# Where the arithmetic of three early norms is done: from GpSimd to VectorE in a four-layer graph kernel

## The reference

```python
def _layernorm(x, axis=-1, eps=1e-5):
    m = jnp.mean(x, axis=axis, keepdims=True)
    v = jnp.var(x, axis=axis, keepdims=True)
    return (x - m) / jnp.sqrt(v + eps)

h = jnp.maximum(_layernorm(x, axis=-1), 0.0)
x = x + _L0_gnn_ref(h, adj, ...)   # layers 1, 2 and 3 in the same way
```

## Time and profile before

| | |
|---|---|
| three runs | 955.87, 958.55, 958.57 us; median 958.55 |
| the profiled execution | 956.38 us, its span 954.7 us |
| instructions in the span | 21094 |
| TensorE matmul | busy 904.9 us (95%) |
| VectorE | busy 834.0 us (87%) |
| ScalarE | busy 758.2 us (79%) |
| GpSimd | busy 416.2 us (44%) |
| mean granted TensorE clock | 0.988 of full speed |

### The profile page before, as it was taken

One profiled execution on the slowest core, in us unless ns is written; L12 is line 12 of the kernel. 1 busy time (PEld: TensorE's weight loads), 2 busy tenths in 40 slices (PEclk: granted clock), 3 DMA queues, 4 the chain that ended last, 5 costly groups with the idle time before them and its releaser, 6 DMA issues. The chain is left out here.

```text
span 954.7 us, 21094 instructions
## 1 busy us (share of the span) xinstructions
PE 904.9 (95%) x7027; PEld 856.7 (90%) x7027; DVE 834.0 (87%) x2599; ACT 758.2 (79%) x2048; POOL 416.2 (44%) x1123
## 2 busy tenths in 40 slices
PE   5878999999999899999999999999999999999998
PEld 4767999999899799999989989999998999898987
DVE  7678899998878999988999898999999888889964
ACT  4798769778589876798778798898678779689863
POOL 5723256233545522363452376444344526354320
PEclk9979999999999999999999999999999999999999
DMA  5200000000110010011000103000100100000013
GB/s 141 68 2 2 2 2 2 1 2 1 46 45 3 2 46 1 2 45 46 2 1 2 45 2 89 2 1 2 45 2 1 46 1 2 1 2 1 1 46 89
DMA packets 43052, 20.05 MB, mean 21 GB/s; under 512 B 8248, under 2 KB 42432, under 8 KB 42944
## 3 DMA queue, kind: packets, MB, share of 16 engines
q1 hardware_dynamic: 41216, 17.97, 6.9%
q10 hardware_dynamic: 1728, 0.73, 0.3%
HBM read 10.17 MB, written 8.39 MB: 19 GB/s over the span
## 5 line engine op out<-in xcount | busy, mean ns | idle before, releaser
L558 PE MATMUL ps<-HE,PT 128*128 128x129 f32 x2048 | 237.3, 275 | 0.6 <-issue 0.3
L558 PEld LDWEIGHTS ps<-HE,PT 128*128 128x128 f32 x2048 | 232.6, 192 | 1.7 <-issue 1.0
L503 ACT ACTIVATE Y<-X,SM 128x128 f32<-128x128 f32 x512 | 203.9, 491 | 21.6 <-POOL SM L499 21.0
L484 POOL TENSOR_TENSOR SM<-ST 128x8 f32<-128x8 f32 x96 | 29.7, 309 | 369.8 <-DVE ST L1329 369.8
L1475 DVE SCALAR_TENSOR_TENSOR PT<-ps,CE,maskT 128x512 f32<-128x512 f32 x256 | 174.2, 744 | 10.5 <-PE ps L715 5.7
L495 POOL TENSOR_TENSOR SM<-SM,minus_half 128x8 f32<-128x8 f32 x96 | 164.6, 1714 | 7.6
L558 PE MATMUL ps<-W,HT 128*128 128x128 f32 x768 | 112.2, 276 | 2.2 <-ACT HT L950 2.0
L1329 DVE BATCH_NORM_STATS2 ST<-X 128x6 f32<-128x128 f32 x512 | 104.8, 279 | 9.5 <-DMA X<-in_x_dram 6.6
L558 PEld LDWEIGHTS ps<-W,HT 128*128 128x128 f32 x768 | 100.5, 192 | 7.0 <-issue 3.0
L601 PE MATMUL ps<-ident,Y 128*128 128x128 f32 x512 | 70.2, 281 | 6.8 <-ACT Y L503 6.6
L601 PEld LDWEIGHTS ps<-ident,Y 128*128 128x128 f32 x512 | 59.9, 145 | 10.7 <-ACT Y L503 9.0
(11 more groups left out here) (263 smaller groups left out, 2199.6 us busy)
## 6 DMA issues: line engine op xcount, KB each, us to landing
X<-in_x_dram SPq DMA_DIRECT2D x32, 256.0 KB, 3.5
out_dram<-X SPq DMA_DIRECT2D x32, 256.0 KB, 2.8
UP<-US SPq DMA_DIRECT2D x64, 2.0 KB, 1.8
adj_raw<-in_adj_dram ACTq DMA_DIRECT2D x2, 256.0 KB, 3.2
adj_raw<-in_adj_dram SPq DMA_DIRECT2D x2, 256.0 KB, 3.8
W<-in_L_gnn_W_dram SPq DMA_DIRECT2D x2, 64.0 KB, 2.8
W<-in_L_gnn_W_dram SPq DMA_DIRECT2D x1, 128.0 KB, 2.4
feat0w<-L_gnn_others_weight_dram ACTq DMA_DIRECT2D x1, 64.0 KB, 4.2
```

Source lines behind the costliest of these rows:

```text
L484: TT(sm[:, S_DIF, :], st[:, :, 1], st[:, :, 4], ALU.subtract)
L503: a = nc.scalar.activation(dst[:, n, 0:F], src[:, n, 0:F], func, scale=SM[s][:, S_RSTD, n:n + 1], bias=SM[s][:, S_SHIFT, n:n + 1])
L558: return nc.tensor.matmul(o, w, m, start=start, stop=stop, skip_group_check=True)
```

## The change

For groups 0, 1 and 2 (`u.group < NS // 2`) VectorE does not stop at the `bn_stats` sums. A new function `variance` goes on to the mean and to the variance itself (with eps, times 0.25 at the end, where `rstd_of` leaves four times it), and its last instruction signs `sig["var"]`. GpSimd then has the power, which now gives the scale directly, and the shift. For the other thirteen groups, and for all later norms, nothing changes. The order of the steps and the PSUM banks are as they were.

```diff
                 def rstd(u, name, s):
                     pool.wait_ge(sig["var"][s], count(u.g, NLN, ln_at[name]))
-                    rstd_of(pool, link, s, name == "gat1").then_inc(sig["rstd"][s], 1)
+                    if name == "norm0" and u.group < NS // 2:
+                        sm = SM[s]
+                        link(TT(sm[:, S_RSTD, :], sm[:, S_VAR, :], minus_half[:], ALU.pow))
+                        TT(sm[:, S_SHIFT, :], sm[:, S_RSTD, :], sm[:, S_MEAN, :], ALU.mult).then_inc(sig["rstd"][s], 1)
+                    else:
+                        rstd_of(pool, link, s, name == "gat1").then_inc(sig["rstd"][s], 1)
...
                 def stat0(u, s):
                     dve.wait_ge(x_loaded[s], (u.g + 1) * 16 * G)
-                    stat(u, s)
+                    if u.group < NS // 2:
+                        variance(u, s)
+                    else:
+                        stat(u, s)
+
+                def variance(u, s):
+                    TT, TS, sm, st = V.tensor_tensor, V.tensor_scalar, SM[s], ST[s]
+                    for n in range(TG):
+                        a = V.bn_stats(st[:, n, :], X[s][:, n, :])
+                    link(a)
+                    TT(sm[:, S_DIF, :], st[:, :, 1], st[:, :, 4], ALU.subtract)
+                    TT(sm[:, S_Q, :], st[:, :, 2], st[:, :, 5], ALU.add)
+                    link(TT(sm[:, S_SUM, :], st[:, :, 1], st[:, :, 4], ALU.add))
+                    TT(sm[:, S_DD, :], sm[:, S_DIF, :], sm[:, S_DIF, :], ALU.mult)
+                    TS(sm[:, S_Q, :], sm[:, S_Q, :], 4.0 / F, 4.0 * LN_EPS, ALU.mult, ALU.add)
+                    link(TS(sm[:, S_MEAN, :], sm[:, S_SUM, :], -0.5, None, ALU.mult))
+                    link(TT(sm[:, S_VAR, :], sm[:, S_Q, :], sm[:, S_DD, :], ALU.add))
+                    TS(sm[:, S_VAR, :], sm[:, S_VAR, :], 0.25, None, ALU.mult).then_inc(sig["var"][s], 1)
```

## The result

The changed kernel takes 960.34 us in the median of 22 runs (959.9 to 962.8), the kernel before 957.61 in 22 runs beside it. The ratio is 1.0036, with a 95% interval of 1.0029 to 1.0043: some 3.4 us (the two medians lie 2.7 apart), against a forecast of +1.7. The profiled execution has a span of 958.4 us, 3.7 more than the earlier trace rows. Of the runs in this text one, in experiment 7, took 1526.93 us at a mean granted clock of 0.558; it is left out of that ratio.

What follows compares the result with a forecast made beforehand. Nearly full TensorE from 100 us on, so early delays move the end; the start hangs on SP's X load. 0 (GpSimd) + 3.3 (VectorE) - 1.6 (slack) = +1.7 us, 958.55 to 960.2 us; range 956.8 to 962.6.

Steps and rivals of the forecast that it cites:

- the rival of full steps: VectorE, groups 0 to 2: each of the eight new instructions costs a full linked step; +3.5 us, chance 0.08.
- GpSimd's relief is worth nothing: GpSimd, groups 0 to 2: the 24 instructions leaving it bring results earlier that nobody waits for; gain 0.
- `biases` and `egin` start some 0.6 us earlier, also for nobody: Next on GpSimd's list after group 1's shift: both start some 0.6 us earlier; worth 0.
- VectorE's 1.1 us a group: VectorE, groups 0 to 2: eight instructions and four links add 1.1 us a group, 3.3 us for three.
- The sign changes over, slack 1.6: SP's X load: `edge["rows"]`, some 1.6 us early, replaces `edge["rank"]` as last wait; loads leave 1.7 us later.
- So I add nothing: Contention of new VectorE instructions beside GpSimd's power: only the power stretches, so 0 was added.
- the clock, which stood as a rival at 0.10: TensorE's gap between `erank` and `eoffm`: clock falls to 1.2 GHz, `eat` 0.9 us later; +2.6 us, chance 0.10.
- it is absorbed: Between 40 and 100 us a wait on something unshifted swallows the 1.7 us; no change, chance 0.12.

Runs made afterwards that it cites:

- experiment 7: The change with `stat0` of group 2 moved behind `erow` on VectorE; ratio to the kernel before 0.9997 (0.9984 to 1.0009).
- Experiment 3: Kernel before with GpSimd making power and shift straight from `bn_stats` columns for groups 0 to 2, nobody computing the variance; ratio 0.9993 (0.9982 to 1.0005).
- experiment 2: The change's VectorE part alone: VectorE does `variance`, GpSimd still does all ten of its instructions; ratio to the kernel before 1.0031 (1.0019 to 1.0044).
- experiment 5: The change with GpSimd's `biases` waiting for `edge["rows"]`; ratio to the kernel before 1.0025 (1.0012 to 1.0038).
- experiments 1: The change for group 1 alone, groups 0 and 2 as in the kernel before; ratio 1.0011 (1.0002 to 1.0020).
- 9: The change with 14 matmuls ahead of `norm0` of group 0 and `stat0` of group 2 behind `erow`; ratio to the kernel before 1.0006 (0.9993 to 1.0019).
- experiment 6: The change with `biases` waiting for `edge["rows"]` and matmuls added on TensorE ahead of `eoffm` and between its groups; ratio to the kernel before 1.0006 (0.9994 to 1.0018).
- experiments 8: Kernel before, without the change, with 14 matmuls ahead of `norm0` of group 0 and `stat0` of group 2 behind `erow`; ratio 0.9986 (0.9975 to 0.9997).
- 10: Kernel before with 14 matmuls ahead of `norm0` of group 0, `stat0` of group 2 behind `erow`, and 8 matmuls ahead of `ecover`; ratio 0.9983 (0.9970 to 0.9995).
- experiment 4: The change with 11 matmuls of 512 columns added on TensorE between `erank` and `eoffm`; ratio to the kernel before 1.0021 (1.0009 to 1.0034).

## Why the forecast was right in its way and half in its size

The measured loss, 2.7 us by the medians and 3.4 by the ratio, lies above the forecast's own range of +1.1 to +2.4; it is inside the whole range because that reached up to the rival of full steps, +3.5, and that rival did not happen. That the median, 960.34 us, lies 0.1 from the 960.2 named is luck: the forecast started from the median of three runs, 958.55, and the kernel before has 957.61 in 22.

**GpSimd's relief is worth nothing: right**, and a little too kind. Experiment 3 shows 0.9993 for the kernel before. Beside late sums the relief does shorten a wait of ScalarE (its idle time ahead of `scale0` of group 1 is 1.63 us in experiment 2 and 0.54 in the change), in a stretch where nothing on the way to `eat` hung on it. What was costed at 0 ("`biases` and `egin` start some 0.6 us earlier, also for nobody") has a price: the end of `erow` is 0.8 us longer beside it.

**VectorE's 1.1 us a group: right.** The step from one group's sums to the next is 2.68 us (11.87 to 14.55) instead of 1.55. Three are 3.4, but 0.42 comes back because the idle time ahead of group 1 shrank from 0.66 to 0.24, so `off_col` is 2.93 late, not 3.3.

**The sign changes over, slack 1.6: right.** 29.21 less 27.51 is 1.70; the sign itself took 0.03, so 1.67. Experiment 7 takes the change-over back, and the loss is no longer to be told.

**The term that was mis-sized is "So I add nothing".** I had weighed the new instructions against GpSimd's power, where the row was right: the three that start beside it (16.22 to 16.40) keep 0.17 us. I did not ask what GpSimd would do beside the old ones once it was done earlier. `edge["rows"]` came 3.80 late for 3.3, and SP 2.13 for 1.7. Experiments 2 and 5 show it both ways. The Trainium skill (GPSIMD Engine Reference, Key points) says that GpSimd contends with VectorE instructions of two SBUF inputs. The trace agrees for `row_ofT`, which has two, beside `biases`: 2.29 against 1.67 us. Beside the power it does not show it on VectorE: `row_ofT` took 1.68 us there in the kernel before, and the new 128x8 instructions 0.17.

**And the clock, which stood as a rival at 0.10.** It came in the profile of the change and in those of experiments 1, 2, 3, 5, 7 and 9, each with a gap ahead of `eoffm`. Its price was worked out as +0.9 on top of the delay; measured at `eat` it is 2.0 (4.29 less 2.30), because the clock stayed low for some 7 us, not 4. That is the larger half of the miss in the profiles. It needs both: in experiment 3 the clock falls and nothing is lost, since TensorE begins 2.9 us earlier than in the change. From 43 us on the shift was handed down: 4.25 at 92.8 us (97.02 less 92.77), 4.15 at the first `att` tile, 3.7 in the span.

**Whether "it is absorbed" had something in it is not shown.** With clock and contention removed, 1.6 us at 40 us become 1.0006 at the end (experiment 6), but 1.6 us would be 1.0017, which the interval still holds. The profiles show one thing between 40 and 100 us that is not fixed: from some 96 us on the clock was at half for about 3.5 us in the kernel before and in the change (there from 100 us), for some 7 and 10 us in experiments 8 and 10, and not at all in 6. Each is one execution.

The sum for the two profiled executions, on the forecast's own terms: 2.9 for VectorE, 0.87 for contention, less 1.67 of slack, 2.1 at the load, 0.2 more at the landing, 2.0 for the clock, less 0.6 given back later: 3.7, the difference of the spans.

## What to carry to other kernels

Before work is moved onto an engine, look which sign stands behind it in that engine's list and how late that sign may come; the same 24 instructions cost 3.4 us ahead of `edge["rows"]` and nothing that could be told (0.9984 to 1.0009) once another step made room. A relieved engine starts its next work earlier: ask beside what. And where a delay opens a gap on TensorE, price the half clock for the work behind the gap, as far as the trace shows it low, not for the gap.

## What the runs showed of the hardware that was not expected

- TensorE's clock fell from 2.4 to 1.2 GHz in the `eoffm`/`eedge` stretch or just ahead of it in all seven profiles whose gap ahead of `eoffm` was not filled (the change and experiments 1, 2, 3, 5, 7 and 9), after 0.24 us (experiment 3) as after 4.05 (experiment 5). In the three without a gap (before, 8, 10) it was 1.00 from 28 to 34 us. `eoffm` is 16 matmuls of one column each; filled ahead but not between (experiment 4) the clock fell later, filled between as well (experiment 6) it stayed up. Whether it is the gap that brings the clock down where it is as small as 0.24 us stays open.
- A VectorE instruction of two SBUF inputs on 128x256 took 0.57 us instead of 0.42 (2.29 and 1.67 for four) beside GpSimd's one-partition instructions; GpSimd's 128x8 instructions beside it, power and all, left it at 0.42 (the kernel before, experiment 2). There it was GpSimd that gave way: its L498, 0.24 us elsewhere, took 0.85 beside `row_of`.
- Two VectorE instructions of 128x8 that read every sixth element start 0.08 to 0.09 us apart, hardly more than the 0.07 of contiguous ones.
